# A GRU scan that starts the candidate's product from an early, rounded r and adds the remainder by a three-slot scan on VectorE

## The chip, the core and the metric

The kernel runs on one NeuronCore of a Trainium2 chip. The metric is the device time of one execution in microseconds, lower is better. Engines: TensorE (PE; its weight loads, PEld, overlap its matmuls), VectorE (DVE), ScalarE (ACT), GpSimd (POOL), and SyncE (SP), which here only starts DMAs.

## The reference

Input x is 16 x 128 x 128 (batch, time, channel). Cut to what matters:

```
x = x + ffn0(gelu(x W^T + bias + low-rank term of each batch row))     # ternary weights, 128 -> 512 -> 128
for t in range(128):                                                   # over time, H is 16 x 128
    Z = sigmoid(x_t Wxz^T + bxz + H Whz^T + bhz)
    R = sigmoid(x_t Wxr^T + bxr + H Whr^T + bhr)
    H~ = tanh(x_t Wxh^T + bxh + (R * H) Whh^T + bhh)
    H = Z * H + (1 - Z) * H~
    Y_t = H Whq^T + bhq
out = x + expert(Y), the expert chosen per token by argmax(Y router^T + router_b)   # 32 experts, 128 -> 32 -> 128
```

The 128 steps over time depend on each other; all else can be done for many tokens at once.

## The kernel before

Channels lie on the 128 partitions, so a state H is a tile of 128 x 16. Time is cut into K = 8 chunks of STEPS = 16 steps (N = 256 tokens). All of it is one Python program that writes out, for each engine, its own queue in order; semaphores (`wait_ge`, `then_inc`) tie the queues. Each engine runs its queue strictly in order.

**Precision.** A product with near-f32 result is made of f16 parts: weights `gru_hi` and `gru_lo`, operands `_p[..., 0, :]` (high part) and `_p[..., 1, :]` (the remainder). `product(out, gate, part)` (lines 976 to 981) issues two matmuls of 16 columns for a high part (weights low, then high) and with `low=True` one for a remainder. They add up in PSUM on top of the input's share and the biases, which are there before the chunk begins (`project`, `project_bias`).

**One step** (k, t), spread over three engines, with p = t % 2:

- TensorE (from line 1126): adds to r's and z's sums the products of z*h (`zh_p`) and of m = (1 - z) * tanh (`m_p`); the new state is z*h + m and is not multiplied itself. In order: r with zh_hi, zh_lo, m_hi; z with zh_hi, zh_lo, m_hi; then r and z with m_lo. Later it adds the products of r*h (`rh_p`) to the candidate's sum.
- ScalarE (from line 447): Sigmoid of r in place in PSUM (line 450), of z (453), of -z (`keep`, 454), Tanh of the candidate in place (481).
- VectorE (from line 740): `rh_hi` (742), `rh` in f32 (743), `zh_hi` (745), `rh_lo` = rh - rh_hi (747), `zh` (749), `zh_lo` (751); then, after the Tanh, `m_hi` (779), `m` in f32 (780, counted by `m_full`), `m_lo` (782), and the new state (784), which is stored in `hist`.

**Background work** fills the gaps of the steps by a timetable written out by hand over k and t. In chunk k it makes for chunk k + 1 the FFN (`ffn_hidden`, `ffn_out`, `ffn_low`, `x1_evacuate`) and the input's projection (`project`, t = 14 and 15), for chunk k + 2 and k + 3 the pre-activation (`pre_full`, `low_rank`, `pre_low_rank`: f32 matmuls), and for chunk k - 1 the outputs: `whq` (Y), `router_logits`, `best_logit`, `best_places` and `first_place` (argmax and masks), `expert_hidden`, `expert_offset`, `expert_low`, `expert_out` for the eight blocks of experts (from t = HIDDEN_AT[c] = 6 + c), and `finish`. On VectorE it stands in two places: small or half-size operations between `zh_lo` and `m_hi`, and the wide ones (128 x 256) behind the new state. On TensorE it stands before the product of `rh_hi`, between that and the product of `rh_lo`, and behind it. `keep_streaming` (line 1048) fills steps with little work with unused matmuls of 256 columns, up to three at a place.

**PSUM.** Eight banks of 512 f32 columns: R0, R1, ZH0, ZH1 for the gates of even and odd chunks, F0, F1 and O for hidden and output sums of FFN and experts, L for low rank, logits and masks. `whq` writes Y to F1. In the bank O only the first 256 columns are used, but for the unused matmuls of chunk 7.

## Time and profile before

| | |
|---|---|
| median of 3 runs | 267.52 us (266.13 to 267.97) |
| span of the profiled execution, first to last instruction | 264.7 us |
| own outer time of the profiled execution | not given on the page |
| instructions | 8,919 |
| busy: TensorE matmul, weight load, VectorE, ScalarE, GpSimd | 238.4, 173.2, 225.5, 127.7, 15.7 us |
| mean granted TensorE clock | 0.993 |

The profile is of one execution. Busy times count pipelined instructions as overlapping, so a share of 90% does not mean that the engine worked at its peak. In a timeline each row has its start and its duration; "x2" after the shapes is two instructions merged in a row.

### The profile page before, as it was taken

How to read it: one execution, taken by the hardware profiler on the slowest of the kernel's cores; microseconds unless marked ns; L12 is line 12 of the kernel's file. 1: busy time of each engine (PE TensorE's matmuls, PEld its weight loads, DVE VectorE, ACT ScalarE, POOL GpSimd, SP SyncE). 2: the span in 40 equal slices, each digit the busy share in tenths (PEclk: the TensorE clock that was granted, in tenths of full speed). 3: DMA queues.
4: the chain of work that ended last, by engine and by line, in shares of the span. 5: the costliest groups of instructions: out<-in, count | busy, mean ns of one | idle time of the engine just before them, and what ended most of it. 6: DMA issues, size and time to landing. Idle time of an engine off the chain costs nothing.

```text
span 264.7 us, 8919 instructions
## 1 busy us (share of the span) xinstructions
PE 238.4 (90%) x3115; PEld 173.2 (65%) x3115; DVE 225.5 (85%) x1540; ACT 127.7 (48%) x698; POOL 15.7 (6%) x29
## 2 busy tenths in 40 slices
PE   7999999999989998999989998999898888888896
PEld 6887666667665676657665676657565656665675
DVE  3779999998999889989999889988989887878864
ACT  3355654654455444654455444654446443434442
POOL 4873000000000000000000000000000000000000
PEclk9999999999999999999999999999999999999979
DMA  7900000000000000000000000000000000000000
GB/s 252 350 10 5 0 4 2 0 4 0 4 24 0 4 2 17 8 2 0 4 22 0 4 4 0 24 2 0 4 24 0 4 0 4 22 1 4 0 22 22
DMA packets 3372, 5.65 MB, mean 21 GB/s; under 512 B 568, under 2 KB 2128, under 8 KB 3328
## 3 DMA queue, kind: packets, MB, share of 16 engines
q1 hardware_dynamic: 2848, 4.24, 4.5%
q10 hardware_dynamic: 432, 0.74, 0.8%
q8 instruction: 25, 0.41, 0.6%
q14 instruction: 19, 0.16, 0.2%
q0 software_dynamic: 48, 0.10, 0.1%
HBM read 4.03 MB, written 1.05 MB: 19 GB/s over the span
## 4 chain that ended last, share of the span: by engine, by line
PE 49%; DVE 31%; ACT 11%; issue 7%; DMA 1%
PE ZH L981 8%; DVE rh_p L742 7%; PE R L980 7%; ACT R L450 7%; PE R L981 7%; PE ZH L980 6%; DVE m_p L779 6%; DVE zh_p L751 3%; ACT ZH L481 3%; DVE rh_p L747 3%; DVE zh_p L745 2%; DVE rh L743 2%; DVE zh L749 2%; PE F L910 2%; PE R L1003 2%
## 5 line engine op out<-in xcount | busy, mean ns | idle before, releaser
L450 ACT ACTIVATE R<-R 128x16 f32<-128x16 f32 x128 | 21.5, 168 | 64.3 <-PE R L981 62.3
L481 ACT ACTIVATE ZH<-ZH 128x16 f32<-128x16 f32 x128 | 21.5, 168 | 55.2 <-PE ZH L981 54.5
L981 PE MATMUL ZH<-rh_p,gru_hi 128*128 128x16 f16 x256 | 45.0, 176 | 0.6
L981 PE MATMUL R<-m_p,gru_hi 128*128 128x16 f16 x254 | 44.6, 176 | 0.0
L981 PE MATMUL ZH<-m_p,gru_hi 128*128 128x16 f16 x254 | 37.3, 169 | 0.0
L980 PEld LDWEIGHTS ZH<-rh_p,gru_lo 128*128 128x128 f16 x128 | 12.3, 96 | 33.6 <-DVE rh_p L742 28.7
L981 PEld LDWEIGHTS ZH<-rh_p,gru_hi 128*128 128x128 f16 x256 | 24.5, 96 | 14.6 <-DVE rh_p L747 0.2
L980 PE MATMUL ZH<-rh_p,gru_lo 128*128 128x16 f16 x128 | 21.7, 169 | 11.0 <-DVE rh_p L742 0.3
L742 DVE TENSOR_TENSOR rh_p<-R,hist 128x16 f16<-128x16 f32 x128 | 22.4, 175 | 9.4 <-ACT R L450 3.2
L779 DVE TENSOR_TENSOR m_p<-keep,ZH 128x16 f16<-128x16 f32 x128 | 21.9, 171 | 9.6 <-ACT ZH L481 8.4
L980 PE MATMUL R<-m_p,gru_lo 128*128 128x16 f16 x127 | 22.9, 180 | 6.1 <-DVE m_p L779 0.2
L1052 PE MATMUL R<-gru_hi 128*128 128x256 f16 x109 | 26.4, 270 | 0.0
L751 DVE TENSOR_TENSOR zh_p<-zh,zh_p 128x16 f16<-128x16 f32 x128 | 22.5, 176 | 4.4
L782 DVE TENSOR_TENSOR m_p<-m,m_p 128x16 f16<-128x16 f32 x128 | 22.4, 175 | 4.4
L981 PEld LDWEIGHTS R<-m_p,gru_hi 128*128 128x128 f16 x254 | 24.6, 97 | 2.0
L981 PE MATMUL ZH<-zh_p,gru_hi 128*128 128x16 f16 x254 | 24.7, 169 | 0.0
L981 PE MATMUL R<-zh_p,gru_hi 128*128 128x16 f16 x254 | 24.7, 169 | 0.0
L454 ACT ACTIVATE keep<-ZH 128x16 f32<-128x16 f32 x128 | 24.3, 190 | 0.0
L981 PEld LDWEIGHTS ZH<-m_p,gru_hi 128*128 128x128 f16 x254 | 24.2, 97 | 0.0
L593 DVE SCALAR_TENSOR_TENSOR hid_lo<-F,hid_hi 128x256 f16<-128x256 f32 x56 | 23.4, 418 | 0.0
L453 ACT ACTIVATE z_sb<-ZH 128x16 f32<-128x16 f32 x128 | 22.8, 178 | 0.3 <-PE ZH L867 0.3
L980 PE MATMUL ZH<-zh_p,gru_lo 128*128 128x16 f16 x127 | 22.9, 181 | 0.0
(251 smaller groups left out, 795.8 us busy)
## 6 DMA issues: line engine op xcount, KB each, us to landing
w_sb<-w SPq DMA_DIRECT2D x2, 512.0 KB, 7.8
outT<-res SPq DMA_DIRECT2D x7, 128.0 KB, 1.9
xs_sb<-xsT SPq DMA_DIRECT2D x1, 640.0 KB, 9.9
first_sb<-first ACTq DMA_DIRECT2D x1, 279.0 KB, 3.7
ffn_sb<-ffn SPq DMA_DIRECT2D x1, 256.0 KB, 3.4
ffn_sb<-ffn ACTq DMA_DIRECT2D x1, 256.0 KB, 4.6
second_sb<-second SPq DMA_DIRECT2D x1, 256.0 KB, 4.2
xs_sb<-xsT SPq DMA_DIRECT2D x1, 256.0 KB, 6.3
```

Source lines behind the costliest of these rows:

```text
L450: nc.scalar.activation(r_io, r_io, ACT.Sigmoid).then_inc(r_made, 1)
L453: nc.scalar.activation(z_sb[:, p, :], z_in, ACT.Sigmoid).then_inc(z_made, 1)
L454: nc.scalar.activation(keep[:, p, :], z_in, ACT.Sigmoid, scale=-1.0).then_inc(keep_made, 1)
L481: nc.scalar.activation(c_io, c_io, ACT.Tanh).then_inc(cand_made, 1)
L593: nc.vector.scalar_tensor_tensor(out=hid_lo[:, c % 4, :], in0=F_bank[c % 2][:, 0:N], scalar=0.0, in1=hid_hi[:, c % 4, :], op0=ALU.max, op1 ...
L742: nc.vector.tensor_tensor(rh_p[:, p, 0, :], r_now, h_old, ALU.mult).then_inc(rh_hi, 1)
L751: nc.vector.tensor_tensor(zh_p[:, q, 1, :], zh[:, q, :], zh_p[:, q, 0, :], ALU.subtract).then_inc(zh_lo, 1)
L779: nc.vector.tensor_tensor(m_p[:, q, 0, :], keep[:, p, :], cand, ALU.mult).then_inc(m_hi, 1)
L782: nc.vector.tensor_tensor(m_p[:, q, 1, :], m[:, q, :], m_p[:, q, 0, :], ALU.subtract).then_inc(m_lo, 1)
L980: mm(out, gru_lo[:, WHR + gate, :], part, start=False, stop=False, skip_group_check=True)
L981: return mm(out, gru_hi[:, WHR + gate, :], part, start=False, stop=low, skip_group_check=True)
L1052: mm(out, gru_hi[:, WHR, :], gru_hi[:, WHZ:WHZ + 2, :], start=False, stop=False, skip_group_check=True)
```

## The change

**An early r.** `early_r` is the unused half of bank O. At each step but the first, TensorE sums there the bias's high part, the input's share (`early_input`: in chunk 0 one f32 matmul of 16 columns, later three f16 ones), and, with the high weights only, zh_hi and m_hi (`early_product`). The early product of m_hi goes ahead of all others of m_hi. ScalarE takes a Sigmoid of it into `r_early` before the exact one, and VectorE makes the high part of r*h from `r_early`.

**The remainder.** `factors` holds for each step and batch row three slots (0, h, exact r), `terms` three slots (-1, 0, the high part of early r*h). One `tensor_tensor_scan` over 48 elements, state = state * factor - term, gives 1, then h, then r*h - high part: the remainder in f16. It replaces `rh` and `rh_lo`. `factors` also replaces `hist` as the store of states (33 places for two chunks; at the end of every odd chunk but the last the state is written twice).

**VectorE's order.** Wide operations still stand behind the new state, and so before the next early product; `zh_lo` moves behind the small background operations, and at t = 0 and 6 (chunk 0: 3 and 12, chunk 7: 0, 10 and 15) the wide one stands before `zh_lo` as well. Several are moved by a step; `best_places` for both halves falls in one step.

**TensorE.** Six matmuls of 16 columns more in a step (four in chunk 0); background work moved by a step here and there; waits for `zh_hi` and `early_made` added; `whq` writes to bank L. `x1_hi` and `x1_lo` have two buffers. VectorE sets `factors` and `terms` at the start.

```
-LAST_HIDDEN_AT = [4, 5, 6, 7, 9, 10, 11, 12]
+LAST_HIDDEN_AT = [5 + c for c in range(8)]
...
+        factors = sb("factors", [128, 2 * STEPS + 1, B, 3])
+        terms = sb("terms", [128, 2, B, 3], F16)
+        parts = sb("parts", [128, 2, B, 3], F16)
+        early_r = O_bank[:, N:2 * N]
+        y_ps = L_bank[:, 0:N]
...
# ScalarE, one step
                     act.wait_ge(r_mm, step + 1)
-                    nc.scalar.activation(r_io, r_io, ACT.Sigmoid).then_inc(r_made, 1)
+                        act.wait_ge(early_mm, step)
+                        nc.scalar.activation(r_early[:, p, :], early_r[:, at], ACT.Sigmoid).then_inc(early_made, 1)
...
+                    nc.scalar.activation(factors[:, step % (2 * STEPS), :, 2], r_in, ACT.Sigmoid).then_inc(r_made, 1)
...
# VectorE, start
+            nc.vector.memset(factors[:], 0.0).then_inc(slots_set, 1)
+            nc.vector.memset(terms[:], 0.0).then_inc(slots_set, 1)
+            dve.wait_ge(slots_set, 2)
+            nc.vector.memset(terms[:, :, :, 0], -1.0).then_inc(slots_set, 1)
...
# VectorE, one step
+                    dve.wait_ge(early_made, step + 1)
+                    dve.wait_ge(h_made, step + 1 + step // (2 * STEPS))
+                    nc.vector.tensor_tensor(terms[:, p, :, 2], r_early[:, p, :], h_old, ALU.mult).then_inc(rh_hi, 1)
                     dve.wait_ge(r_made, step + 1)
-                    dve.wait_ge(h_made, step + 1)
-                    nc.vector.tensor_tensor(rh_p[:, p, 0, :], r_now, h_old, ALU.mult).then_inc(rh_hi, 1)
-                    nc.vector.tensor_tensor(rh[:, p, :], r_now, h_old, ALU.mult).then_inc(rh_full, 1)
+                    dve.wait_ge(rh_hi, step + 1)
+                    nc.vector.tensor_tensor_scan(parts[:, p].rearrange("p b s -> p (b s)"),
+                                                 factors[:, now].rearrange("p b s -> p (b s)"),
+                                                 terms[:, p].rearrange("p b s -> p (b s)"), 0.0,
+                                                 ALU.mult, ALU.subtract).then_inc(rh_lo, 1)
                     dve.wait_ge(z_made, step + 1)
                     nc.vector.tensor_tensor(zh_p[:, q, 0, :], z_sb[:, p, :], h_old, ALU.mult).then_inc(zh_hi, 1)
-                    dve.wait_ge(rh_full, step + 1)
-                    nc.vector.tensor_tensor(rh_p[:, p, 1, :], rh[:, p, :], rh_p[:, p, 0, :],
-                                            ALU.subtract).then_inc(rh_lo, 1)
                     nc.vector.tensor_tensor(zh[:, q, :], z_sb[:, p, :], h_old, ALU.mult).then_inc(zh_full, 1)
...
+                    elif not last and k > 0 and t in (0, 6):
+                        wide(k, t)
...
+                    dve.wait_ge(zh_full, step + 1)
+                    nc.vector.tensor_tensor(zh_p[:, q, 1, :], zh[:, q, :], zh_p[:, q, 0, :],
+                                            ALU.subtract).then_inc(zh_lo, 1)
...
+                    if now == 2 * STEPS - 1 and not last:
+                        nc.vector.tensor_tensor(factors[:, 0, :, 1], zh[:, q, :], m[:, q, :],
+                                                ALU.add).then_inc(h_made, 1)
...
# TensorE
+            def early_input(k, t):
+                out, at = early_r[:, t * B:(t + 1) * B], slice(t * B, (t + 1) * B)
+                mm(out, gbias[:, 0:C], ones16[:, 0:B], start=False, stop=False, skip_group_check=True)
+                if k == 0:
+                    mm(out, gru_sb[:, WXR, :], x1[:, at], start=False, stop=False, skip_group_check=True)
+                else:
+                    hi, lo = x1_hi[:, k % 2, at], x1_lo[:, k % 2, at]
+                    for w, a in ((gru_lo, hi), (gru_hi, hi), (gru_hi, lo)):
+                        mm(out, w[:, WXR, :], a, start=False, stop=False, skip_group_check=True)
+            def early_product(t, part):
+                return mm(early_r[:, t * B:(t + 1) * B], gru_hi[:, WHR, :], part, start=False, stop=False,
+                          skip_group_check=True)
...
                     if step > 0:
+                        pe.wait_ge(zh_hi, step)
+                        product(r_out, 0, zh_p[:, q, 0, :])
+                        if out_bank_read(k, t - 1):
+                            pe.wait_ge(zh_lo, step)
+                        early_input(k, t)
+                        early_product(t, zh_p[:, q, 0, :])
                         pe.wait_ge(zh_lo, step)
-                        product(r_out, 0, zh_p[:, q, 0, :])
                         product(r_out, 0, zh_p[:, q, 1, :], low=True)
                         pe.wait_ge(m_hi, step)
+                        early_product(t, m_p[:, q, 0, :]).then_inc(early_mm, 1)
                         product(r_out, 0, m_p[:, q, 0, :])
...
-                    product(c_out, 2, rh_p[:, q, 0, :])
+                    product(c_out, 2, terms[:, p, :, 2])
...
-                    product(c_out, 2, rh_p[:, q, 1, :], low=True).then_inc(cand_mm, 1)
+                    product(c_out, 2, parts[:, p, :, 2], low=True).then_inc(cand_mm, 1)
```

## Rows read from the trace of the kernel before

**Rows 1.** The page: busy time of each engine, and the chain by engine.

```profile
PE 238.4 (90%) x3115; PEld 173.2 (65%) x3115; DVE 225.5 (85%) x1540; ACT 127.7 (48%) x698; POOL 15.7 (6%) x29
...
PE 49%; DVE 31%; ACT 11%; issue 7%; DMA 1%
```

**Rows 2.** The view by source line, line 481 (Tanh).

```profile
L481 ACT ACTIVATE ZH<-ZH x128: 168/168/168, 14.9 to 254.3; 128x16 f32<-128x16 f32 x128
```

**Rows 3.** Timeline of one step in chunk 3: start, duration (us), engine, line.

```profile
120.69 0.17 DVE L779 TENSOR_TENSOR m_p<-keep,ZH 128x16 f16<-128x16 f32 x1
120.78 0.16 DVE L780 TENSOR_TENSOR m<-keep,ZH 128x16 f32<-128x16 f32 x1
...
120.92 0.18 PE L980 MATMUL R<-m_p,gru_lo 128*128 128x16 f16 x1
...
120.97 0.17 DVE L782 TENSOR_TENSOR m_p<-m,m_p 128x16 f16<-128x16 f32 x1
...
121.06 0.17 DVE L784 TENSOR_TENSOR hist<-zh,m 128x16 f32<-128x16 f32 x1
...
121.15 0.42 DVE L593 SCALAR_TENSOR_TENSOR hid_lo<-F,hid_hi 128x256 f16<-128x256 f32 x1
...
121.20 0.18 PE L981 MATMUL R<-m_p,gru_hi 128*128 128x16 f16 x1
...
121.42 0.17 ACT L450 ACTIVATE R<-R 128x16 f32<-128x16 f32 x1 [0.48 <-PE R L981]
...
121.62 0.17 DVE L742 TENSOR_TENSOR rh_p<-R,hist 128x16 f16<-128x16 f32 x1
...
121.72 0.16 DVE L743 TENSOR_TENSOR rh<-R,hist 128x16 f32<-128x16 f32 x1
...
121.91 0.17 DVE L747 TENSOR_TENSOR rh_p<-rh,rh_p 128x16 f16<-128x16 f32 x1
...
122.14 0.18 PE L981 MATMUL ZH<-rh_p,gru_hi 128*128 128x16 f16 x1
...
122.36 0.17 ACT L481 ACTIVATE ZH<-ZH 128x16 f32<-128x16 f32 x1 [0.61 <-PE ZH L981]
...
122.44 0.38 ACT L382 ACTIVATE hid_hi<-F 128x256 f16<-128x256 f32 x1
...
122.56 0.17 DVE L779 TENSOR_TENSOR m_p<-keep,ZH 128x16 f16<-128x16 f32 x1
```

**Rows 4.** Busy time by stretch: chunk 0, chunk 3, chunk 7 without its end.

```profile
14.85:45.24 30.39, 27.85 (x359) 21.17 (x360) 27.61 (x191) 17.51 (x93) 6.28 (x13) 1.00 0.01 3
...
105.43:135.54 30.11, 27.61 (x373) 19.62 (x372) 27.15 (x190) 15.09 (x86) 0.00 (x0) 1.00 0.02 7
225.93:254.27 28.34, 24.93 (x347) 17.23 (x346) 23.32 (x173) 11.38 (x72) 0.00 (x0) 1.00 0.02 7
```

**Rows 5.** Timeline behind the last step: two wide VectorE operations.

```profile
254.94 0.42 DVE L627 SCALAR_TENSOR_TENSOR hid_last_lo<-R,hid_last_hi 128x256 f16<-128x256 f32 x1
...
255.27 0.42 DVE L627 SCALAR_TENSOR_TENSOR hid_last_lo<-ZH,hid_last_hi 128x256 f16<-128x256 f32 x1
```

**Rows 6.** Timeline of TensorE in chunk 2, t = 11.

```profile
94.72 0.17 PE L980 MATMUL ZH<-zh_p,gru_lo 128*128 128x16 f16 x1
94.75 0.19 PE L981 MATMUL ZH<-zh_p,gru_hi 128*128 128x16 f16 x2
...
94.93 0.47 PE L988 MATMUL L<-xs_sb,first_sb 128*128 128x128 f32 x2
95.23 0.27 PE L833 MATMUL F<-y_hi,w_lo 128*128 128x256 f16 x1
95.34 0.27 PE L834 MATMUL F<-y_hi,w_hi 128*128 128x256 f16 x1
```

**Rows 7.** The view by source line, line 574 (`best_places`): duration in ns.

```profile
L574 DVE SCALAR_TENSOR_TENSOR key<-L,top,const_sb x14: 243/244/249, 48.9 to 228.6; 128x32 f32<-128x32 f32 x14
```

**Rows 8.** Timeline of VectorE at the start, with its wait.

```profile
4.26 0.69 DVE L670 TENSOR_REDUCE asum<-ffn_sb 128x1 f32<-128x512 f32 x1 [3.04 <-DMA ffn_sb<-ffn]
```

More of the change, by code:

```diff
@@ L726, in first_late, with wide @@
                     g_low(1)
+                if 8 <= t < 8 + NF:
+                    ffn_low(1, t - 8)
                 if t == 12:
+                    dve.wait_ge(xs_next_in, 16)
+                    x1_evacuate(1)
+                if t == 14:
                     x1_low(1)
+            def wide(k, t):
+                if t == 0 and k == 1:
+                    w1_low(3)
+                if t == 0 and k > 1:
+                    finish(k - 2)
+                if t == 1:
+                    y_low(k - 1)
+                if 2 <= t < 2 + NF:
+                    ffn_low(k + 1, t - 2)
+                if t == 6:
+                    if k == 2:
+                        dve.wait_ge(xs_in, 16)
+                    x1_evacuate(k + 1)
+                if 7 <= t < 15:
+                    expert_low(k - 1, t - 7)
@@ new lines, in wide_last @@
+            def wide_last(t):
+                if t == 0:
+                    finish(K - 3)
+                if t == 1:
+                    y_low(K - 2)
+                if t == 2:
+                    best_logit(K - 2)
+                if t == 3:
+                    first_place(K - 2, 0)
+                    first_place(K - 2, 1)
+                if t - 1 in LAST_HIDDEN_AT:
+                    expert_low(K - 2, LAST_HIDDEN_AT.index(t - 1))
+                if t == 10:
+                    last_best_places(0)
+                if t == 15:
+                    finish(K - 2)
@@ L1156, in _ @@
                         low_rank(k + 3, 0)
[L1157 to L1158 removed]
+                    if feed and 3 <= t - late < 3 + NF:
+                        if k == 0 and t == 3 + late:
                             pe.wait_ge(wq16_made, 2)
                             pe.wait_ge(x1_rest_made, 1)
[L1161 removed]
+                        pe.wait_ge(early_made, step + 1)
+                        ffn_out(k + 1, t - late - 3)
                     if 0 < k < K - 2 and t == 9:
```

233 lines of the change are left out of this document (121 added, 112 removed).

## The prediction

> **What bounds the kernel now.** I read the shares of the engines and the chain that ended last first. TensorE is busy for 90% of the span and the chain gives it 49%, with 7% "issue" [rows 1]. Taken alone that says "TensorE is full". The second view contradicts it: the Tanh of line 481 runs once in each of the 128 steps of the recurrence, from 14.9 to 254.3 us [rows 2], so 127 steps take 239.4 us, 1.885 us each. The stretches show it to be nearly constant: 30.39 us for chunk 0, 30.11 for a middle chunk and 28.34 for the 15 steps before the last Tanh [rows 4], whatever background work a chunk carries. A period that ignores the load is a chain of latencies, so I read one step in order of time [rows 3], counted from the start of `m_hi` (line 779) at 120.69:
>
> - `m_hi` 0, `m_full` 0.09, `m_lo` 0.28 (it needs `m_full`), new state 0.37, a wide background operation 0.46;
> - the exact r's last product on TensorE 0.51, its Sigmoid 0.73 (+0.22), `rh_hi` 0.93 (+0.20);
> - `rh` 1.03, and `rh_lo` 1.22, which needs `rh`; `rh_lo`'s product 1.45 (+0.23), Tanh 1.67 (+0.22), next `m_hi` 1.87 (+0.20).
>
> The sum is 1.87 against 1.885. So the bound is this ring; the other work lies in its gaps.
>
> **The change, part by part.** *Early r.* A second PSUM strip gets r's input cheaply, with the f16 high parts, so a rounded r*h exists early. After `m_hi` only one product is missing. TensorE gets it at 0.23 (today's 120.92 [rows 3]); +0.22 gives the early Sigmoid at 0.45, +0.20 `rh_hi` at 0.65. VectorE has issued the new state at 0.37; where a wide operation follows at 0.46 it stands in front. How long it holds the engine is read from two wide operations on ready data: 254.94 and 255.27, 0.33 apart though each lasts 0.42 [rows 5]. I take 0.36. So `rh_hi` starts at 0.82 with a wide operation before it and at 0.65 without.
>
> *The scan.* It waits for the exact r (Sigmoid at 0.73, so 0.93) and for `rh_hi`: a dependent operation starts 0.20 after its source, as `m_full` to `m_lo` [rows 3]. So it starts at 1.02 behind a wide operation, at 0.93 otherwise. Its duration stands in no row. Bounds: 0.17 (16 elements, line 742) and 0.42 (256 elements, line 593) [rows 3]; a straight line between them gives 0.20 for its 48 elements. I take 0.25, by the row nearest in kind: a 32-element operation that carries a sum along, 0.244 [rows 7]. Then +0.06 to TensorE, as after line 747, +0.22 Tanh, +0.20 `m_hi`: 1.02 + 0.25 + 0.06 + 0.42 = **1.75 us** behind a wide operation, and 1.66 (I take 1.67) without, against 1.885.
>
> The Trainium skill (DVE: opcode table, instruction layouts, handler registers and perf-mode slots; section 6, Datapath and trigger behaviour) says that the built-in scan feeds its result back to an earlier stage and so runs at half throughput. By that, an estimate, the 48 elements cost twice their 0.05 us over the fixed part, 0.25; by the straight line it would be 0.20, which over 128 steps makes 252.5 us. No row here shows a scan.
>
> *What goes.* `rh` and the subtraction (lines 743, 747) leave the ring: 0.29 between `rh_hi` and `rh_lo` gives way to the scan, of which only about 0.08 is longer than the subtraction; the rest of the gain is that `rh_hi` no longer waits for the exact r.
>
> *Slots between.* `zh_lo` now comes behind the narrow background operations, and `m_hi` behind it. Scan 1.02, `zh_hi` 1.19, `zh` 1.28, `zh_lo` 1.48, engine free at 1.57: before the 1.75 at which `m_hi` may start. A half-size operation (0.28, holding 0.20) still fits. What does not fit: `best_places` twice in one slot, about 0.25 each [rows 7], `zh_lo` at 1.9, next `m_hi` at 2.0: +0.25 once in a chunk. A full-size operation in that slot at t = 6 and t = 0 puts `m_hi` at 1.84 and 1.77: +0.11 together. In chunk 7, t = 10 puts a maximum, `expert_low` and `best_places` there: +0.5.
>
> *TensorE.* Each step gets six more matmuls of 16 columns: bias, three for the input, two products. Small ones are issued 0.025 to 0.03 apart [rows 6]: +0.16 us in a step. A light expert step holds 22 matmuls: 15 small ones 0.41, seven of 256 columns at 0.11 [rows 6] 0.77, together 1.18, so 1.34 of 1.75. Hidden by the gaps, if they stand in the right place. Between `rh_lo`'s product and the next need, 0.64 before `m_hi`'s product, it must issue `expert_out` 0.33 and eight small ones 0.22: it fits with 0.09 over. It does not fit at t = 9, 10 and 11 of chunks 1 to 4 and t = 9 and 10 of chunk 5, where an f32 matmul of 128 columns (0.30: the row "x2" is one of them in two passes [rows 6]) stands in each half of the step: 21 x 0.027 + 0.77 + 0.62 = 1.96 of TensorE. Followed from step to step: at t = 9 the product of `m_hi` comes about 0.25 late, the exact r's last 0.19 late, and the intervals become about 1.80, 1.99, 1.99 and 1.85 until it has caught up, +0.63 over four times 1.75, and without t = 11 +0.39: 2.91 in all, 0.49 per middle chunk. Two waits grow: `ffn_out` for `ffn_low`, whose wide operation ends at 0.88 (four steps, +0.1 together), and the logits for `y_low` (+0.07). `y_low` and the second copy of the state at every second chunk: +0.06 and +0.05.
>
> *Chunk 0.* The early input is an f32 matmul here; bounds 0.05 (two small ones) and 0.30 (128 columns [rows 6]), and I take the upper, since its weights are as large: 0.38 more per step with three small ones. Steps 0 to 4 are full of f32 work already: five at 2.0, eleven at 1.80 (`m_hi`'s product 0.1 late), 29.8 against 30.4.
>
> *Start and end.* A fill of 1,584 f32 elements and two small ones join VectorE's start: 128 partitions of this at about 1 ns an element is 1.7 us, beneath its 3.04 us wait for the weights [rows 8]; uncovered it would cost 1.7. ScalarE gets one Sigmoid more, 0.17, in the 0.48 it idles before line 450 [rows 3]. Its queue reaches the early one in time: a wide one behind the Tanh starts 0.12 before `m_hi` and ends at 0.26, before 0.45. The end after the last Tanh keeps its 10.4 us. The DMAs are the same.
>
> **Sum.** Middle chunk: 14 x 1.75 + 2 x 1.67 = 27.84; + 0.25 + 0.11 + 0.06 + 0.05 + 0.07 + 0.10 + 0.49 = 28.97, against 30.1: 1.13, six times 6.8. Chunk 7: 15 x 1.75 + 0.25 + 0.5 + 0.1 = 27.1 against 28.34: 1.2. Chunk 0: 0.6. Together 8.6 less. The profiled execution spans 264.7, and would span 256.1; the page gives no outer time for it, and the median of the three runs, 267.52, lies 2.8 above the span. So **258.9 us**.
>
> **Rivals.**
> *A, slower: the scan is dear.* Every step has it on the ring. It has eaten the gain at 0.25 + 8.6/128 = 0.32 us. At the upper bound 0.42 it adds 0.17 x 128 = 22: 281 us. For it: no row shows one, and elements that hang on each other can't overlap. Against: it has only 48.
> *B, no change: a wide operation holds VectorE to its end.* Today the next operation starts 0.47 after it (121.15 to 121.62 [rows 3]). Were that the engine's own, `rh_hi` would start at 0.93, the scan at 1.13, +0.11 in some 90 steps that TensorE does not bind already, +9.9: 269 us. Against: at 121.62 r has just become ready, and the pair of [rows 5] stands 0.33 apart.
> *C, smaller gain: TensorE binds in all expert steps.* The margin of 0.09 is one matmul of 256 columns. If each of 56 expert steps loses 0.1: 264.5 us. For: 90% busy. Against: the same period for light and heavy steps.
> *D, smaller gain: spread operands.* States, factors and terms lie 12 or 6 bytes apart. The cost per element is about 1.04 ns, from (417 - 170)/240; doubled for 16 elements that is 0.017 an operation, with two or three on the ring 0.04 a step: 264 us. The Trainium skill (SBUF — State Buffer, on SBUF "cachelines") says that accesses crossing to a new 16-byte line pay a penalty and gives no number for it; today's trace has no such operand on the ring.
>
> **How the numbers follow.** Forecast 0.55 (its own range 252.5 to 263), A 0.13, B 0.12, C 0.10, D 0.10. A scan at 0.20 takes the time to 252.5, one at 0.30 to 265.3; the range is 252 to 266, which leaves A and B outside. Faster by over 1% (about what a measurement of this kernel can tell from no change): 0.55 + 0.10 + 0.10 = 0.75; within 1%: 0.12; slower: 0.13.
>
> **What would show it.** Tanh to Tanh near 1.75 in ordinary steps of the middle chunks; scan duration 0.25; `rh_hi` starting 0.8 after `m_hi` behind a wide operation; the exact Sigmoid still at 0.73; TensorE back to back at t = 9 to 12 with steps of 1.8 to 2.0; one longer step at t = 3 to 4. Wrong it would be with a scan over 0.32 us, with the exact r's last product later than 0.55 in ordinary steps, or with the Tanh waiting for something other than the scan's product.

## The result, and the profile after

| | |
|---|---|
| after, median of 7 runs | 269.8 us (269.18 to 276.66) |
| before, same chip, median of 7 runs | 267.35 us (265.95 to 268.01) |
| ratio | 1.0104, 95% interval 1.0064 to 1.0143 |
| span after, mean granted TensorE clock | 267.9 us, 0.98 |
| predicted | 258.9 us (252 to 266), faster |

The change costs 1%; the forecast was 3% faster, and the time lies outside the range. Four of the seven executions of after ran at a mean granted clock of 0.98 (269.2 to 269.8 us) and three at 0.937 to 0.949 (274.6 to 276.7 us), and the ratio is of the four. The traces below are each of one execution, and their granted clock is told where it matters.

The page of after, its engines and the chain by engine:

```profile
PE 241.3 (90%) x3873; PEld 196.9 (73%) x3873; DVE 219.3 (82%) x1418; ACT 149.3 (56%) x826; POOL 15.3 (6%) x29
...
PE 56%; DVE 25%; ACT 9%; issue 7%; DMA 1%; DVEq 0%
```

Against [rows 1], VectorE has 6 us less and its share of the chain falls from 31% to 25%, while TensorE's rises from 49% to 56%. That is a first hint that TensorE took over. The Tanh, now line 490, runs from 14.6 to 258.4 us, which answers to [rows 2], and the stretches answer to [rows 4] (chunks 0, 3, 6 and 7, the last without its end, bounds rounded to 0.1 us; then 2 us inside chunk 7; columns: stretch, length, busy TensorE, weight load, VectorE, ScalarE and GpSimd, granted clock, DMA):

```profile
14.60:47.10 32.50, 29.25 (x440) 24.42 (x441) 26.77 (x174) 20.12 (x109) 6.06 (x14) 1.00 0.01 3
...
107.60:137.80 30.20, 27.81 (x471) 22.60 (x469) 26.05 (x175) 17.82 (x102) 0.00 (x0) 1.00 0.02 7
198.30:229.50 31.20, 27.93 (x459) 22.15 (x458) 25.16 (x169) 17.38 (x100) 0.00 (x0) 0.95 0.02 7
229.50:258.40 28.90, 26.20 (x436) 20.55 (x435) 22.86 (x158) 13.88 (x88) 0.00 (x0) 0.88 0.03 7
240.00:242.00 2.00, 1.92 (x29) 1.44 (x28) 1.50 (x11) 0.96 (x6) 0.00 (x0) 0.50 0.00 0
```

| stretch, Tanh to Tanh | before | predicted | after |
|---|---|---|---|
| start, to the first Tanh | 14.85 | 14.85 | 14.62 |
| chunk 0 | 30.39 | 29.8 | 32.50 |
| chunks 1 to 5, each | 30.1 | 28.97 | 30.21 to 30.29 |
| chunk 6 | 30.2 | 28.97 | 31.17 |
| chunk 7, 15 intervals | 28.34 | 27.1 | 28.93 |
| last Tanh to the end | 10.4 | 10.4 | 9.5 |

The whole miss lies in the steps: 2.7 us in chunk 0, 8.6 in chunks 1 to 6, 1.8 in chunk 7, less 1.1 at the two ends. (The last end is shorter because the two profiled executions differ in TensorE's clock there: 0.82 in the last 11 us of before, 0.97 in the last 10 of after. It is no gain of the change that any run shows.) In chunk 3 the 16 intervals after are 1.80, 1.87, 1.82, 1.82, 1.84, **2.17**, 1.81, 1.87, 1.87, 1.90, 1.91, 1.91, 1.87, 1.89, 1.82, **2.04**. Before they were all near 1.88. The period does now depend on the load: the ring (the chain of operations that depend on each other from one `m_hi` to the next) is shorter in a light step, and steps with something extra give the gain back.

One ordinary step, chunk 3, t = 2 to 3, answers to [rows 3]. The timeline of after:

```profile
111.46 0.17 DVE L852 TENSOR_TENSOR m_p<-keep,ZH 128x16 f16<-128x16 f32 x1
...
111.69 0.18 PE L940 MATMUL O<-m_p,gru_hi 128*128 128x16 f16 x1
...
111.91 0.18 ACT L456 ACTIVATE r_early<-O 128x16 f32<-128x16 f32 x1
111.93 0.41 DVE L562 TENSOR_TENSOR hid_lo<-hid,hid_hi 128x256 f16<-128x256 f32 x1
...
112.20 0.19 ACT L460 ACTIVATE factors<-R 128x16 f32<-128x16 f32 x1
...
112.26 0.18 DVE L799 TENSOR_TENSOR terms<-r_early,factors 128x16 f16<-128x16 f32 x1
...
112.34 0.19 ACT L463 ACTIVATE keep<-ZH 128x16 f32<-128x16 f32 x1
...
112.54 0.26 DVE L804 TENSOR_TENSOR_SCAN parts<-factors,terms 128x48 f16<-128x48 f32 x1
...
112.71 0.17 PE L1064 MATMUL ZH<-terms,gru_lo 128*128 128x16 f16 x1
...
112.76 0.27 PE L1142 MATMUL R<-gru_hi 128*128 128x256 f16 x1
...
112.87 0.18 PE L1065 MATMUL ZH<-parts,gru_hi 128*128 128x16 f16 x1
...
113.08 0.17 ACT L490 ACTIVATE ZH<-ZH 128x16 f32<-128x16 f32 x1 [0.18 <-PE ZH L1065]
...
113.28 0.17 DVE L852 TENSOR_TENSOR m_p<-keep,ZH 128x16 f16<-128x16 f32 x1
```

Counted from `m_hi` at 111.46, with the forecast in brackets: early product 0.23 (0.23), early Sigmoid 0.45 (0.45), exact Sigmoid 0.74 (0.73), `rh_hi` behind a wide operation 0.80 (0.82), scan 1.08 (1.02) with duration 0.26 (0.25), remainder's product 1.41 (1.33), Tanh 1.62 (1.55), next `m_hi` 1.82 (1.75). Two things are off. The scan starts 0.28 behind `rh_hi` though a dependent operation was priced at 0.20. And TensorE is not free when the scan comes: `rh_hi` was made by 112.44, but its product starts at 112.71, 0.18 after `keep` ended (112.53), which it also waits for, and behind it stands a matmul of 256 columns (112.76, holding TensorE 0.11), so the remainder's product could start at 112.87 at the earliest, whatever the scan did.

One step of after shows TensorE's part alone. At t = 6 of chunk 3 no wide operation stands before `rh_hi`, so the scan starts already at 0.96, and its product could follow at 1.28:

```profile
120.07 0.26 DVE L804 TENSOR_TENSOR_SCAN parts<-factors,terms 128x48 f16<-128x48 f32 x1
...
120.32 0.17 PE L1064 MATMUL ZH<-terms,gru_lo 128*128 128x16 f16 x1
...
120.48 0.17 PE L1065 MATMUL ZH<-parts,gru_hi 128*128 128x16 f16 x1
```

The product comes at 1.37, behind a matmul of 256 columns at 120.38, and this step still takes 1.81.

### The profile page after: what moved, and what is told of

The parts are those of the page before. It is cut to its first block, busy times and chain, and to the rows that moved or that the text cites. A ratio compares the mean times of both kernels' runs of the same rounds, so it can differ in the third digit from the quotient of the medians.

```text
span 267.9 us, 10598 instructions
## 1 busy us (share of the span) xinstructions
PE 241.3 (90%) x3873; PEld 196.9 (73%) x3873; DVE 219.3 (82%) x1418; ACT 149.3 (56%) x826; POOL 15.3 (6%) x29
## 4 chain that ended last, share of the span: by engine, by line
PE 56%; DVE 25%; ACT 9%; issue 7%; DMA 1%; DVEq 0%
PE ZH L1065 5%; PE ZH L1064 4%; PE R L1065 4%; PE F L896 4%; DVE hid_lo L604 3%; DVE m_p L855 3%; DVE m_p L852 3%; ACT ZH L490 3%; PE R L1142 3%; PE O L940 3%; DVE parts L804 2%; ACT factors L460 2%; PE F L994 2%; PE L L962 2%; DVE terms L799 2%
## 5 line engine op out<-in xcount | busy, mean ns | idle before, releaser
L804 DVE TENSOR_TENSOR_SCAN parts<-factors,terms 128x48 f16<-128x48 f32 x128 | 33.1, 259 | 13.9 <-ACT factors L460 0.5
L456 ACT ACTIVATE r_early<-O 128x16 f32<-128x16 f32 x127 | 23.2, 183 | 36.7 <-PE O L940 34.2
L1065 PE MATMUL R<-zh_p,gru_hi 128*128 128x16 f16 x254 | 41.5, 170 | 0.1
L460 ACT ACTIVATE factors<-R 128x16 f32<-128x16 f32 x128 | 24.5, 191 | 9.1
L1064 PEld LDWEIGHTS ZH<-terms,gru_lo 128*128 128x128 f16 x128 | 12.5, 97 | 23.0 <-DVE terms L799 18.7
L799 DVE TENSOR_TENSOR terms<-r_early,factors 128x16 f16<-128x16 f32 x128 | 23.4, 183 | 6.8 <-ACT r_early L456 4.3
L1064 PE MATMUL ZH<-terms,gru_lo 128*128 128x16 f16 x128 | 22.3, 174 | 7.0 <-ACT keep L463 2.0
L1065 PEld LDWEIGHTS R<-zh_p,gru_hi 128*128 128x128 f16 x254 | 24.7, 97 | 2.2 <-DVE zh_p L848 0.2
L931 PE MATMUL O<-ones,gbias 128*128 128x16 f16 x127 | 21.7, 171 | 2.4 <-DVE zh_p L848 2.3
L1065 PE MATMUL ZH<-parts,gru_hi 128*128 128x16 f16 x128 | 22.7, 177 | 0.6 <-DVE parts L804 0.2
```

Source lines behind the costliest of these rows:

```text
L456: nc.scalar.activation(r_early[:, p, :], early_r[:, at], ACT.Sigmoid).then_inc(early_made, 1)
L460: nc.scalar.activation(factors[:, step % (2 * STEPS), :, 2], r_in, ACT.Sigmoid).then_inc(r_made, 1)
L799: nc.vector.tensor_tensor(terms[:, p, :, 2], r_early[:, p, :], h_old, ALU.mult).then_inc(rh_hi, 1)
L804: nc.vector.tensor_tensor_scan(parts[:, p].rearrange("p b s -> p (b s)"), factors[:, now].rearrange("p b s -> p (b s)"), terms[:, p].rearr ...
L1064: mm(out, gru_lo[:, WHR + gate, :], part, start=False, stop=False, skip_group_check=True)
L1065: return mm(out, gru_hi[:, WHR + gate, :], part, start=False, stop=low, skip_group_check=True)
```

## The experiments

**Is it the scan?** A scan that takes 0.26 where 0.25 was counted leaves rival A little room, but its start might have a price. The first kernel puts back the two operations of before, from the exact r:

```diff
-tensor_tensor_scan(parts, factors, terms, 0.0, mult, subtract)      # waits: r_made, rh_hi
+rh = factors[..., 2] * h_old                                         # wait: r_made
 zh_hi = z * h_old
+parts[..., 2] = rh - terms[..., 2]                                   # waits: rh_hi, rh_full
```

> The scan is replaced by two plain VectorE operations on the same operands: rh = exact r times h in f32, then rh minus the early high part; z*h's high part stands between them, as in the kernel before. Theory 1 (the scan starts late behind rh_hi: 0.28 us instead of the 0.20 of two dependent plain operations, and lasts 0.26): rh starts 0.93 after m_hi, the subtraction 1.13, its product on TensorE 1.36 instead of 1.41, so ordinary steps with a wide operation fall from 1.82 to 1.77 and the total by about 3 us. Rival (the spread 6-byte and 12-byte operands make any reader late, scan or not): the subtraction too starts 0.28 behind its source, its product comes at 1.44, and nothing is gained or 2 us are lost.

283.35 us (281.09 to 286.2), ratio 1.0621 (1.0533 to 1.0710), clock of the profiled run 0.976; ordinary steps 1.91. Both the theory (3 us less) and its rival (at most 2 us more) missed: the two operations with their waits are dearer than the scan. Rival A, a scan of 0.32 us or more, falls by the scan's own duration of 0.26. The timeline of VectorE in this kernel shows where the time goes:

```profile
121.59 0.18 DVE L805 TENSOR_TENSOR rh<-factors 128x16 f32<-128x16 f32 x1
...
121.88 0.19 DVE L810 TENSOR_TENSOR parts<-rh,terms 128x16 f16<-128x16 f32 x1
```

From `rh` to the subtraction it is 0.29 (median of the 128 steps 0.28), where before had 0.19 with the same operation between (121.72 to 121.91 [rows 3]). This subtraction, as the scan, has two waits in front of it; that of before had one.

The second kernel puts `zh_hi` between `rh_hi` and the scan, so that both waits of the scan are met before it is reached:

```diff
 rh_hi = r_early * h_old
+zh_hi = z * h_old                                                    # wait: z_made
 tensor_tensor_scan(...)                                              # waits: r_made, rh_hi
-zh_hi = z * h_old
```

> z*h's high part is issued between rh_hi and the scan; nothing else changes. It can start when z's Sigmoid is done, about 1.03 us after m_hi. If the 0.28 from rh_hi to the scan is the time until rh_hi's result can be read, the scan starts 0.09 behind z*h, at 1.12, and 0.32 behind rh_hi. If a scan can start only when the plain operation before it has left the engine, whoever wrote its operands, it starts 0.26 to 0.28 behind z*h, at about 1.30, and steps grow by 0.2 us, 20 us in all.

```profile
121.46 0.18 DVE L803 TENSOR_TENSOR zh_p<-z_sb,factors 128x16 f16<-128x16 f32 x1 [0.17 <-ACT z_sb L462]
...
121.55 0.25 DVE L806 TENSOR_TENSOR_SCAN parts<-factors,terms 128x48 f16<-128x48 f32 x1
```

One run, 272.49 us. The scan starts 0.09 behind `zh_hi`, as two simple operations do. So two waits cost nothing here, where both are met before the scan is reached, and the scan need not wait until the operation before it has ended. `zh_hi` itself waits for z (0.17), so the steps are 1.85.

**Second wait or spread operands?** Three kernels take the suspects apart. In the first the two-operation form loses its wait for `rh_hi`, which VectorE's own wait for the later `rh` covers:

```diff
-dve.wait_ge(rh_hi, step + 1)
 dve.wait_ge(rh_full, step + 1)
```

> As the kernel with two plain operations in the scan's place, whose subtraction started 0.29 us behind rh, but the subtraction now waits for rh alone (line order makes the wait for rh_hi superfluous, as in the kernel before). If the 0.28 to 0.29 comes from two waits ahead of one instruction whose last is on VectorE's own result, the subtraction starts 0.20 behind rh and ordinary steps fall from 1.91 to about 1.83. If it comes from operands 6 and 12 bytes apart, it stays at 0.29 and the steps at 1.91.

```profile
113.03 0.18 DVE L805 TENSOR_TENSOR rh<-factors 128x16 f32<-128x16 f32 x1
...
113.25 0.19 DVE L809 TENSOR_TENSOR parts<-rh,terms 128x16 f16<-128x16 f32 x1
```

One run, 270.9 us at a clock of 0.981, with steps of 1.84 (from 1.91): the distance shrank from 0.29 to 0.22 (medians 0.28 and 0.21) by taking away one line. With one wait the two operations are thus within 0.02 a step of the scan with two. In the second, the wait for the exact r moves ahead of `rh_hi`, which leaves one wait at the scan:

```diff
+dve.wait_ge(r_made, step + 1)
 rh_hi = r_early * h_old
-dve.wait_ge(r_made, step + 1)
 dve.wait_ge(rh_hi, step + 1)
 tensor_tensor_scan(...)
```

> The changed kernel with its scan; the wait for the exact r moves from ahead of the scan to ahead of rh_hi, so the scan waits for rh_hi alone. A measurement of one gap: rh_hi starts at 0.95 after m_hi and the step grows. If two waits make the gap, the scan starts 0.20 behind rh_hi; if the spread 6-byte write of rh_hi or the scan's own reading makes it, 0.28 as before. Steps 1.89 or 1.97 us.

The scan starts 0.23 behind `rh_hi` (126.92 to 127.15) instead of 0.28 (medians 0.22 and 0.28), though the kernel is far slower (one run, 299.57 us, clock 0.919), since `rh_hi` now waits for the exact r; its steps of 2.02 lie above both values expected. The third is the two-operation form with two waits and r, high part and remainder in packed tiles of their own:

```diff
-activation(factors[:, ..., 2], r_in, Sigmoid)
+activation(r_full[:, p, :], r_in, Sigmoid)
-terms[..., 2] = r_early * h_old ; rh = factors[..., 2] * h_old ; parts[..., 2] = rh - terms[..., 2]
+early_hi = r_early * h_old ; rh = r_full * h_old ; early_lo = rh - early_hi
```

> Two plain operations with both waits, but the exact r, the early high part and the remainder lie packed in tiles of their own; only the state stays spread by 12 bytes. If spread operands make the gap, the subtraction starts 0.20 behind rh and steps take 1.83; if two waits do, 0.29 and 1.91.

```profile
115.79 0.18 DVE L808 TENSOR_TENSOR rh<-r_full,factors 128x16 f32<-128x16 f32 x1
...
116.07 0.18 DVE L813 TENSOR_TENSOR early_lo<-rh,early_hi 128x16 f16<-128x16 f32 x1
```

Still 0.28 to 0.29 (one run, 278.14 us, steps 1.89): spreading r, high part and remainder (rival D) has no part in the distance, and next to none in the duration (median of `rh_hi` 0.179 in after, 0.172 here). The state stayed spread in this kernel; before, where it is packed too, has 0.175 for `rh_hi`.

**Take the second wait off the scan itself.** ScalarE's exact Sigmoid counts up the same semaphore as `rh_hi`, and the scan waits once for both:

```diff
-activation(..., Sigmoid).then_inc(r_made, 1)
+activation(..., Sigmoid).then_inc(rh_hi, 1)
-dve.wait_ge(r_made, step + 1)
-dve.wait_ge(rh_hi, step + 1)
+dve.wait_ge(rh_hi, 2 * step + 2)                                     # TensorE waits for this too
```

> The changed kernel with one edit: the exact Sigmoid and rh_hi count the same semaphore, and the scan (and TensorE's product of rh_hi) waits for their sum, so the scan has one wait in place of two. Theory: the scan starts 0.22 behind rh_hi instead of 0.28, so steps with a wide operation in front, not bound by TensorE, go from 1.82 to 1.76; expert steps at t = 7, 12 and 13, bound by TensorE's wait for expert_low, stay at 1.87; about 45 steps gain, 3 us: a ratio to before near 1.00 in runs with a high clock. Rival: TensorE, whose product of rh_hi waits for keep and is followed by a matmul of 256 columns, takes over at once; steps stay at 1.79 or more, less than 1.5 us gained.

```profile
112.11 0.19 DVE L799 TENSOR_TENSOR terms<-r_early,factors 128x16 f16<-128x16 f32 x1
...
112.24 0.19 ACT L463 ACTIVATE keep<-ZH 128x16 f32<-128x16 f32 x1
...
112.33 0.26 DVE L803 TENSOR_TENSOR_SCAN parts<-factors,terms 128x48 f16<-128x48 f32 x1
...
112.57 0.17 PE L1063 MATMUL ZH<-terms,gru_lo 128*128 128x16 f16 x1
112.62 0.27 PE L1141 MATMUL R<-gru_hi 128*128 128x256 f16 x1
112.73 0.17 PE L1064 MATMUL ZH<-parts,gru_hi 128*128 128x16 f16 x1
```

The scan now starts 0.22 behind `rh_hi`, 0.06 sooner, and the light steps barely move: 1.81 for 1.82, chunk 3 30.10 us for 30.21 (0.1 to 0.3 less in the chunks at full clock). The scan is done at 112.59, its product starts at 112.73. `keep` ended at 112.43, the product of `rh_hi` came 0.14 after, then the 256 columns. TensorE was already the second limit, 0.01 a step behind the first. The whole kernel took 273.73 us (ratio 1.0239, 1.0178 to 1.0301), but all four of its executions ran at a clock of 0.937 to 0.961, and chunk 0 alone took 38.07 us at a clock of 0.69. Here the whole time would have misled; the chunk at full clock does not.

**Take TensorE's limit off.** Two edits. VectorE's wide operations of chunks 1 to 6 move out of the way of `rh_hi`, to between `zh` and `zh_lo`, and the narrow ones take their place behind the new state. And TensorE's background work between the two products of r*h moves ahead of its wait for `rh_hi`. One kernel does the first edit, the next both:

```diff
-    elif not last and k > 0 and t in (0, 6):        # wide(k, t) ahead of zh_lo
+    elif not last and k > 0:
...
-    elif k > 0 and not last and t not in (0, 6):    # behind the new state
-        wide(k, t)
+    elif k > 0 and not last:                        # best_logit, best_places, first_place, x1_low, ..., one step sooner
```

> Chunks 1 to 6: VectorE's wide operations move from behind the new state to between zh and zh_lo of the same step, and the narrow ones take the place behind the new state, one step earlier. Theory: the wide operation in front delays rh_hi from 0.65 to 0.80 and with it the scan from 0.96 to 1.08; and TensorE waits in each expert step for expert_low, up to 0.94. With the exchange the scan starts at 0.96 to 0.98, expert steps at t = 7, 12 and 13 lose their 0.05 as well, the next m_hi is set by zh_lo behind the wide operation, at 1.75, and a middle chunk takes 29.0 to 29.4 instead of 30.2 us: 5 to 7 us less in all, about 263 us, if the clock holds. Rival 1: TensorE is the bound already (product of rh_hi only after keep, then a matmul of 256 columns), steps stay at 1.79 to 1.80: 2 us less. Rival 2: zh_lo, now late, holds back TensorE's early input and product, and steps grow over 1.85.

```diff
+expert_offset(...) / project(...) / keep_streaming(...)              # chunks 1 to 7
 pe.wait_ge(rh_hi, step + 1)
 pe.wait_ge(keep_made, step + 1)
 product(c_out, 2, terms[:, p, :, 2])
-expert_offset(...) / project(...) / keep_streaming(...)
```

> As e8_swap (wide and narrow VectorE operations exchanged in chunks 1 to 6), and in chunks 1 to 7 TensorE's work that stood between the products of rh_hi and of the remainder (expert_offset, two projections, one unused matmul) goes ahead of both. Theory: in e8_swap the step is bound by TensorE there: it waits 0.3 us idle for keep, starts the product of rh_hi 1.2 after m_hi, and a matmul of 256 columns keeps the remainder's product until 1.38, though the scan would allow 1.29. With the work ahead, the remainder's product comes at 1.29, steps fall from 1.80 to 1.72 to 1.75, 5 us less than e8_swap's 263.4 at a high clock. Rival: zh_lo behind the wide operation on VectorE holds m_hi at 1.79, nothing gained.

The first: 265.82 us, too spread for a ratio (263.35 and 263.46 at clock 0.993, 268.19 and 268.98 at 0.962); chunk 3 29.39, most light steps 1.80. `rh_hi` is there sooner, `keep` and the 256 columns hold the rest, and the largest single gain is the step t = 5 to 6, from 2.17 to 1.84. The second: 259.17 us (258.60 to 265.39), ratio 0.9700 (0.9639 to 0.9762); chunk 3 28.79, steps without f32 matmuls mostly 1.71 to 1.79. Its timeline at t = 7 of chunk 3:

```profile
117.74 0.19 ACT L463 ACTIVATE keep<-ZH 128x16 f32<-128x16 f32 x1
117.77 0.27 PE L996 MATMUL F<-mask,expand_off 128*128 128x256 bf16 x1
117.82 0.26 DVE L804 TENSOR_TENSOR_SCAN parts<-factors,terms 128x48 f16<-128x48 f32 x1
...
118.08 0.17 PE L1066 MATMUL ZH<-terms,gru_lo 128*128 128x16 f16 x1
...
118.14 0.18 PE L1067 MATMUL ZH<-parts,gru_hi 128*128 128x16 f16 x1
```

The 256-column matmul runs while `keep` is made, and the products of high part and remainder stand next to each other, 0.06 apart. Two limits meet here again: the product of the high part starts 0.15 after `keep` ends and has the remainder's behind it, and the scan ends 0.06 before that one, which comes 1.27 after `m_hi`.

**Both limits, nothing else.** This kernel has the wide operations where the change put them, one wait at the scan, and TensorE's work moved:

> The changed kernel, its wide operations still behind the new state, with two edits: the scan's single wait of e10_one_sem, and TensorE's work ahead of the product of rh_hi as in e9_swap_pe. Theory: two limits lie side by side in the changed kernel, the scan's second wait (steps 1.82) and TensorE between keep and the remainder's product (steps 1.81 in e10_one_sem); only with both gone does an ordinary step reach the forecast 1.75 (t = 2, 3, 14 of the middle chunks), while expert steps stay near 1.87 by the wait for expert_low. Rival: the forecast 1.75 was out of reach for a third reason, and steps stay at 1.79 or more.

262.93 us (262.49 to 263.81), ratio 0.9860 (0.9819 to 0.9901). The steps t = 13 and 14 take 1.75: there `rh_hi` starts at 0.80, the scan at 1.01 and the remainder's product at 1.33, which is the ring as forecast. Chunk 3 takes 29.57 (after 30.21). At t = 2 and 3, where 1.75 was expected as well, and at t = 1 and 4 the steps stay at 1.81. The timeline says why:

```profile
111.96 0.27 PE L913 MATMUL O<-hid_hi,wq 128*128 128x256 f16 x1 [0.18 <-DVE hid_lo L562]
...
112.18 0.27 PE L1141 MATMUL R<-gru_hi 128*128 128x256 f16 x1
112.29 0.17 PE L1063 MATMUL ZH<-terms,gru_lo 128*128 128x16 f16 x1
112.34 0.17 PE L1064 MATMUL ZH<-parts,gru_hi 128*128 128x16 f16 x1
```

TensorE waits for `hid_lo`, the wide operation ahead of `rh_hi`, and three matmuls of 256 columns then come before the products. A kernel with TensorE's work moved and two waits left at the scan, the wide operations in place, was not run; the step t = 6 of after above stands in for it.

**Chunk 0.** Three steps there (t = 3, 4 and 12) take 2.38 to 2.50. The timeline of after shows the waits of the first two:

```profile
21.75 0.18 PE L931 MATMUL O<-ones,gbias 128*128 128x16 f16 x1 [0.36 <-DVE zh_p L848]
...
24.57 0.41 ACT L393 CAST g_hi<-g 128x256 f16<-128x256 f32 x1 [0.94 <-DVE g L545]
```

`zh_lo` stands behind two VectorE operations, and on ScalarE `g_high`, behind the Tanh, waits 0.94 for an operation of VectorE with the early Sigmoid queued behind it (24.88). The step t = 12 has the same kind of wait as t = 3, 0.48 for `zh_lo`. Moving `g_high` one step later:

```diff
-if k == 0 and t == 4: g_high(1)                                      # behind the Tanh
+if k == 0 and t == 5: g_high(1)                                      # ahead of the Tanh; w2_high moved from 5 to 4
```

> In chunk 0 ScalarE's g_high goes back to t = 5, ahead of the Tanh, and the second w2_high to t = 4; in the changed kernel g_high stands behind the Tanh of t = 4, waits 0.94 us for twice_gelu, and the early Sigmoid stands behind it. Theory: the interval from t = 4 to 5 falls from 2.48 to about 1.95 and the total by 0.5 us. Rival: TensorE's f32 work sets that interval anyway, and it stays above 2.3.

By itself it can't be read: 273.35 us (268.42 to 274.66), ratio 1.0134 (1.0042 to 1.0226). From 24 to 40 us TensorE had half its clock, 1.2 GHz, and chunk 0 took 36.77 us. Later traces at full clock say more. In the kernel with both limits off, which keeps `g_high` behind the Tanh, the step from t = 4 to 5 takes 2.48; in the last kernel below, with `g_high` moved and three unused matmuls at the start of step 4, it takes 2.10 (expected was 1.95). And the single wait is worth more in chunk 0 than anywhere else: 31.43 us with it, against 32.50 in after and 32.50 and 32.45 in the two kernels that exchange VectorE's operations with two waits left. Why it gives 1.0 us there is not explained.

**The clock.** In after, two steps of chunk 6 (t = 7, 8) and two of chunk 7 (t = 6, 7) take 2.2 to 2.3, and the window from 240 to 242 us shows TensorE at half clock (0.50). I suspected the idle stretches of TensorE and filled them in chunks 6 and 7:

```diff
+if k >= 6:                                                           # ahead of expert_hidden
+    two unused matmuls of 256 columns
```

> Two unused matmuls of 256 columns go ahead of each expert_hidden in chunks 6 and 7, where TensorE now waits for expert_low; they fit in that wait. Theory: the granted clock falls to 1.2 GHz in chunks 6 and 7 because TensorE idles there in every expert step with no f32 matmuls in between; with the fill the clock stays at 1.00 through both chunks, five steps go from 2.2 to 2.3 us back to 1.87 to 1.93, and the time falls by 2 us against the changed kernel (ratio to before about 1.003) with no runs of 274 us. Rival: the clock falls for a reason that the fill does not touch (the activity over the whole run): clock and time stay as they are, ratio 1.010.

275.22 us (269.93 to 279.27), no ratio. Chunk 6 kept its clock (30.59 us), chunk 7 did not, and in this execution chunks 0, 1 and 3, which the edit does not touch, lost theirs as well (mean clock 0.932). So this edit alone does not hold the clock.

**Together.** All changes that seemed to help, with one to three unused matmuls at idle places (step 4, the expert steps of chunks 6 and 7, `unread_bank` at t < 5), first without TensorE's move:

> e8_swap, the single wait of e10_one_sem, g_high ahead of the Tanh at t = 5 as in e4_g_high, and unused matmuls where TensorE idles and the clock then fell: three ahead of the wait for zh_lo at the start of step 4, one in each expert step of chunk 6, two in those of chunk 7, and three places at t = 4 of chunk 7. Theory: the falls of the granted clock follow TensorE's idle stretches of 0.35 to 0.7 us in chunk 0 (t = 3 to 5) and chunk 7; with both filled the clock stays above 0.99 in all runs, none lies above 264 us, and the median is 260 to 262. Rival: the clock falls in chunk 0 in some runs all the same (0.96, 268 us).

then with it (and without the fill in chunk 6):

> e9_swap_pe with the single wait, g_high ahead of the Tanh at t = 5 of chunk 0, three unused matmuls at the start of step 4, and in chunk 7 two in each expert step and three places at t = 4. Theory: the middle chunks stay as in e9_swap_pe (28.7 us), chunk 0 falls from 32.5 to 31.5, the clock holds in chunk 0 in all runs: 257 to 258 us with no run above 260. Rival: the single wait gives nothing and the unused matmuls cost TensorE as much as the clock gives back: 259 us.

261.48 us (260.79 to 262.22), ratio 0.9792 (0.9746 to 0.9838); and **255.27 us** (254.38 to 255.30), ratio **0.9554** (0.9521 to 0.9587), faster than both kernels. The first lies in its expected range, the second 2 us below it. All eight executions of the two ran at a clock of 1.00. In the second, TensorE is busy for 95% of the span and VectorE for 84%. Its chunks 0 and 3 in the view by stretches:

```profile
15.55:46.62 31.07, 29.16 (x444) 24.90 (x445) 26.66 (x174) 20.24 (x109) 5.08 (x11) 1.00 0.01 3
...
103.71:132.13 28.42, 27.62 (x472) 23.16 (x470) 25.19 (x175) 17.93 (x103) 0.00 (x0) 1.00 0.02 7
```

Most light steps take 1.70 to 1.71, and chunk 7 27.50 us. These steps have no wide operation ahead of `rh_hi`, for which the forecast had 1.67; the scan starts at 0.96, forecast 0.93. Chunk 3, all at clock 1.00, sums the study up:

| kernel | what it has | chunk 3, us |
|---|---|---|
| before | | 30.11 |
| after | the change | 30.21 |
| after, one wait at the scan | first limit off | 30.10 |
| after, wide operations moved | | 29.39 |
| one wait, TensorE's work moved | both limits off | 29.57 |
| wide operations and TensorE's work moved | | 28.79 |
| all | | 28.42 |

## Why the prediction was wrong

**The scan and rival A: right.** 0.259 over 128 scans, forecast 0.25:

```profile
L804 DVE TENSOR_TENSOR_SCAN parts<-factors,terms 128x48 f16<-128x48 f32 x128 | 33.1, 259 | 13.9 <-ACT factors L460 0.5
```

The straight line between 16 and 256 elements, 0.20, was wrong. The Trainium skill (DVE: opcode table, instruction layouts, handler registers and perf-mode slots; section 6, Datapath and trigger behaviour) says that the built-in scan runs at half throughput, and the estimate made from it, 0.25, agrees with the trace; no scan of another length was run that would show the cost per element. **Rival B: false.** `rh_hi` started 0.33 behind a wide operation of 0.41 (111.93 to 112.26). **Rival D: false** for r, high part and remainder by the packed kernel. **The early chain** came at 0.23, 0.45 and 0.80 as forecast.

**"A dependent operation starts 0.20 after its source": wrong for the scan.** This is the first step of the prediction that failed. The scan started at 1.08, not 1.02. With one wait the distance is 0.22, with two 0.28. The price was taken from `m_full` to `m_lo` [rows 3], which has one wait. This step alone gives 1.82 for 1.75: 0.07 in every light step behind a wide operation, had nothing else bound them.

**"Hidden by the gaps, if they stand in the right place" and rival C: the placement was not followed.** This is the second step that failed. The sum of TensorE's work in a step, 1.34 of 1.75, fits in the step, but that was beside the point. The product of `rh_hi` waits for `keep` too (ends 1.07), and a matmul of 256 columns stands between it and the remainder's product. That sets 1.41 for the remainder's product where the forecast had 1.33, as late as the scan does. The wait for `keep` stands in the program of before too, and TensorE waited for it there: in all 128 steps the product of `rh_hi` starts 0.14 to 0.17 after `keep` ends. It cost nothing, because `rh_lo` came later still. The step of [rows 3] one period earlier has it:

```profile
119.69 0.19 ACT L454 ACTIVATE keep<-ZH 128x16 f32<-128x16 f32 x1
...
120.02 0.17 PE L980 MATMUL ZH<-rh_p,gru_lo 128*128 128x16 f16 x1
```

So the trace of before showed the next limit, and the prediction did not list it. C had the right engine with the wrong mechanism: I priced it as 0.1 in 56 expert steps and as the end of the margin before `m_hi`; it was 0.06 to 0.07 in the light steps, at another place. The kernel with both limits off reached 1.75 at t = 13 and 14, so the ring itself was right, and two terms beside it were left out.

**Single steps.** For chunk 3 with its t = 9 to 12 the forecast made 29.11, and 30.21 came. Four places account for it:

- t = 5 to 6, 2.17 against 1.75, +0.42: not in the forecast, which had its one longer step at t = 3 to 4. `first_place` for both halves now stands at t = 5 of VectorE's new slot, so the masks' matmul is late, ScalarE waits 0.36 for it, and the wide mask operation stands in front of the early Sigmoid, at 0.70 instead of 0.45. "Its queue reaches the early one in time" had looked only at operations on ready data. TensorE adds to it: `ffn_out`, which waits for `hid_lo`, and the three matmuls of `expert_hidden` stand ahead of the product of `rh_hi`, and the remainder's product comes 0.27 after the scan has ended (118.40 to 118.67). With `first_place` one step earlier, behind the new state, and the wide operations moved, the step took 1.84.

```profile
117.27 0.47 ACT L374 ACTIVATE mask<-L,const_sb 128x256 bf16<-128x256 bf16 x1 [0.36 <-PE L L981]
...
117.64 0.17 ACT L456 ACTIVATE r_early<-O 128x16 f32<-128x16 f32 x1
```

- t = 15 to 0, 2.04 against 1.80, +0.24. The f32 `whq` starts at 135.90, just before `m_hi` at 135.96, and holds TensorE; small matmuls whose operands were long ready then still stand ahead of the early product (136.53, 0.57 after `m_hi` where 0.23 was counted). The early Sigmoid comes at 0.78. The list of f32 steps had t = 9 to 11 and missed this one. That the f32 matmul is the cause was read from the trace; no run moved it.

```profile
135.90 0.59 PE L962 MATMUL L<-factors,gru_sb 128*128 128x128 f32 x2
...
136.53 0.17 PE L940 MATMUL O<-m_p,gru_hi 128*128 128x16 f16 x1
```

- t = 7, 8 and 13, about 1.88 against 1.75, +0.37 together. There `expert_hidden` waits for the `expert_low` that VectorE has behind the new state of the same step, and its three matmuls of 256 columns then stand ahead of the product of `rh_hi`. The timeline at t = 7 has the instruction that waits:

```profile
121.85 0.28 PE L896 MATMUL F<-y_hi,w_lo 128*128 128x256 f16 x1 [0.21 <-DVE hid_lo L604]
```

- The other seven light steps, +0.10: they are 0.07 to 0.14 longer each than 1.75 or 1.67, 0.69 together, but the forecast had 0.59 of single terms on them, which hardly showed. The largest, +0.25 for the pair of `best_places` in one slot, is not there: that step takes 1.84.

The four f32 steps came to 7.59 against 7.63. Their sum was right, and it is the one place where TensorE was followed from product to product; the single intervals were 1.90, 1.91, 1.91 and 1.87 for 1.80, 1.99, 1.99 and 1.85.

**Chunk 0, +2.7.** "Five at 2.0, eleven at 1.80" was 1.3 us short for the five and 1.4 for the eleven. Three steps of 2.38 to 2.50, from the waits shown above (`g_high`, `zh_lo` behind two operations), make some 1.5 of it. The single wait gave back 1.0, and the last kernel, with `g_high` moved and three unused matmuls besides, 1.4 (31.07).

**Chunk 7, +1.8.** The +0.5 for the full slot at t = 10 came as forecast: 2.03 and 1.99 at t = 10 and 11. Two steps make 1.1 of the miss. The step t = 6 took 2.30 at half clock and 1.85 to 1.87 in the two kernels that kept the clock. The step t = 7 took 2.29, and there it is not the clock, for it takes 2.28 in the last kernel at a clock of 1.00:

```profile
230.01 0.26 DVE L803 TENSOR_TENSOR_SCAN parts<-factors,terms 128x48 f16<-128x48 f32 x1
...
230.28 0.50 PE L1014 MATMUL L<-factors,gru_sb 128*128 128x128 f32 x2
```

The f32 matmul of the last `whq` holds TensorE for 0.33 ahead of the product of `rh_hi`, behind the three of `expert_hidden`: a second f32 step that the forecast's list lacks.

**The clock.** The forecast said nothing of it and took 1.00 throughout. At half clock, three steps (t = 7 and 8 of chunk 6, t = 6 of chunk 7) took 0.3 to 0.4 more each, some 1.2 us in the better executions; the worse ones lost 5 to 7 us more. Without those 1.2 us after would still not be faster than before (268.6 us, an estimate). What makes the clock fall stays open. One thing points to missing unused matmuls. The twelve kept traces of kernels with the change and none of them at t = 4 of chunk 7 all show half clock in chunk 7, for 3 to 10 us, that of the kernel with both limits off included (233.4 to 236.7 us); the two with such matmuls there do not. Another thing points away from it: before, with none at t = 4 either and TensorE busy for 1.68 of 1.89 us in that step, kept its clock there, while the kernel with both limits off was busy for 1.49 of 1.70 and lost it one step later. No kernel had those matmuls as its only edit.

The scan of t = 15 in chunk 6 started 0.63 behind `rh_hi`, and this step took 2.17. It is no accident of one execution: the distance is 0.63 to 0.64 in all five traces that have the scan as in after with its two waits, and 0.21 to 0.30 in the four with the single wait. Why it is so long just there is not explained.

**Sum.** The whole difference adds up as follows: 258.9, + 2.7 + 8.6 + 1.8 for the steps, − 1.1 at the ends, − 0.9 for the time around the span (1.9, counted as 2.8): 270.0, measured 269.8.

## What to carry to other kernels

When a chain of latencies is shortened, the next limit can be very near; here it stood 0.01 us behind the first. For every operation of the new chain write down all its waits and what stands before it in its own queue, with the time of each, and take the latest. With two limits side by side, removing one shows almost nothing (30.21 to 30.10), and removing both shows what the chain can do (29.57, with two steps at the forecast 1.75). An operation that takes its operand from another engine belongs in a queue where that operand is long ready, or it holds the chain's next instruction behind it.

## What was not expected of the hardware

A second semaphore wait ahead of a VectorE instruction cost 0.06 to 0.07 us when VectorE's own preceding result is the one that comes last (0.28 and 0.22 for the scan, 0.29 and 0.22 for the subtraction), and nothing when both had been met before (0.09 behind the operation before). Counting two producers up on one semaphore avoids it. TensorE's granted clock fell to 1.2 GHz for stretches of 3 to 24 us, in some executions and not in others of the same kernel. It cost chunk 0 of 16 steps 5.7 us in one kernel (38.24 in the trace with unused matmuls in chunks 6 and 7, 32.50 in after) and 6.6 in another (38.07 with the single wait, 31.43 with both limits off, which has the same chunk 0 but for two projections). The busy share inside such a stretch (1.92 of 2.00 us) says nothing of the cause, because the matmuls themselves are longer there: one of 256 columns took 0.42 us at 242.87, where most take 0.27.
